# First attention of a decoder block: order of the masked reads, of the e-transposes and of the rstd work around two state scans

## The reference, cut to what matters

```python
q, k, v = heads(x @ Wq, 64), heads(x @ Wk, 64), heads(x @ Wv, 128)
s = clip(heads(x @ Ws, 64), -32, 32)
# scan over t: hk = hk * g_t + k_t p_t ;  ok_t = q_t . hk
pv = softmax(ok)                                   # over the 64 slots
# scan over t: hv = hv * g_t + p_t v_t ;  ov_t = pv_t . hv
o = ov * rsqrt(mean(ov * ov, -1) + 1e-5) * g_norm_weight
o = o * (g * sigmoid(g))                           # g = x @ Wg
out = o @ Wo                                       # added to x, then a layer norm
```

## Time and profile before

| | us |
|---|---|
| three runs | 971.32, 976.60, 978.88 |
| median | 976.6 |
| profiled execution, whole | 978.59 |
| its span (first to last instruction) | 976.7 |

### The profile page before, as it was taken

How to read it: one execution, slowest core, us unless ns; L and a number is a source line. 1 busy time by engine, 2 the same in 40 slices (tenths; PEclk the granted TensorE clock), 3 DMA queues, 4 the chain that set the end, 5 groups by cost and what they waited for, 6 DMA issues and landing times.

```text
span 976.7 us, 15390 instructions
## 1 busy us (share of the span) xinstructions
PE 870.8 (89%) x5247; PEld 569.4 (58%) x5251; DVE 716.3 (73%) x1389; ACT 505.8 (52%) x1020; POOL 407.7 (42%) x338
## 2 busy tenths in 40 slices
PE   7999999999999999989999999999547867999886
PEld 3466666656566666656867776676423654443443
DVE  5677786959686877769765556665577798997897
ACT  3563554545444445445443334455522457898485
POOL 0202448494847667454214343343477303221012
PEclk9999999999999999998799999999866998999998
DMA  5450212211230222100746999999633000000001
GB/s 191 159 194 28 65 49 87 70 66 61 74 103 33 87 71 87 40 5 1 228 141 209 314 314 316 317 302 289 183 92 97 17 1 3 7 7 6 1 6 38
DMA packets 54743, 106.46 MB, mean 109 GB/s; under 512 B 8909, under 2 KB 26645, under 8 KB 54165
## 3 DMA queue, kind: packets, MB, share of 16 engines
q1 hardware_dynamic: 48917, 89.88, 29.4%
q0 software_dynamic: 5760, 15.74, 5.9%
HBM read 88.45 MB, written 17.14 MB: 108 GB/s over the span
## 4 chain that ended last, share of the span: by engine, by line
PE 61%; DVE 17%; DMA 6%; ACT 5%; issue 5%; POOL 3%; SPq 2%; DVEq 0%; ACTq 0%; POOLq 0%
PE ps L785 10%; PE ps L723 7%; PE ps L969 6%; PE ps L881 5%; PE ps L981 4%; PE ps L733 4%; DVE row_max L2757 3%; POOL key_part L1545 3%; PE ps L1317 3%; DVE state L2177 2%; DMA w_dn<-in_w_dn 2%; PE ps L803 2%; DMA y_dram<-y_out 2%; PE ps L1303 2%; PE ps L847 1%
## 5 line engine op out<-in xcount | busy, mean ns | idle before, releaser
L1516 POOL DMA_INDIRECT xg<-x_dram,tok_of x68 | 65.1, 958 | 129.1 <-PE ps L1042 91.4
L785 PE MATMUL ps<-w_vg,xT 128*128 128x512 f32 x256 | 116.8, 597 | 1.2 <-DVE th L2220 1.2
L1466 POOL TENSOR_TENSOR state<-state,rows_bc 128x1024 f32<-128x1024 f32 x22 | 53.8, 2444 | 95.5 <-DVE state L2177 41.9
L723 PE MATMUL ps<-xT,w_qks 128*128 128x512 f32 x192 | 86.6, 596 | 5.9 <-ACT qT L1623 5.3
L969 PE MATMUL ps<-w_gv,xgT 128*128 128x352 f32 (+1 forms) x272 | 87.7, 464 | 2.8 <-DMA w_dn<-in_w_dn 2.7
L2757 DVE TENSOR_REDUCE row_max<-ps 128x4 f32<-128x1024 f32 x64 | 74.4, 1217 | 7.1 <-PE ps L1282 6.3
L2188 DVE TENSOR_TENSOR aT<-ps,tri 128x768 f32<-128x768 f32 x64 | 59.7, 954 | 27.0 <-PE ps L733 26.9
L1623 ACT ACTIVATE probT<-ps 128x512 f32<-128x512 f32 x128 | 69.5, 594 | 10.3 <-PE ps L1303 9.8
L785 PEld LDWEIGHTS ps<-w_vg,xT 128*128 128x128 f32 x256 | 45.8, 190 | 48.8 <-issue 43.1
L981 PE MATMUL ps<-w_dn,hidT 88*128 88x256 f32 (+1 forms) x272 | 69.9, 379 | 0.0
L969 PEld LDWEIGHTS ps<-w_gv,xgT 128*128 128x128 f32 x272 | 48.8, 190 | 27.2 <-issue 5.6
(11 more groups left out here) (328 smaller groups left out, 2064.8 us busy)
## 6 DMA issues: line engine op xcount, KB each, us to landing
w_gv<-in_w_gv SPq DMA_DIRECT2D x68, 352.0 KB, 7.1
rows_bc<-x_dbl_dram SPq DMA_DIRECT2D x32, 512.0 KB, 3.8
w_dn<-in_w_dn SPq DMA_DIRECT2D x68, 192.0 KB, 8.8
y_dram<-y_out SPq DMA_DIRECT2D x68, 128.0 KB, 7.0
y_dram<-blank SPq DMA_DIRECT2D x4, 1408.0 KB, 13.2
w_vg<-in_wvg SPq DMA_DIRECT2D x8, 512.0 KB, 4.9
w_qks<-in_wqks SPq DMA_DIRECT2D x8, 384.0 KB, 3.1
w_o<-in_wo SPq DMA_DIRECT2D x8, 256.0 KB, 2.7
```

The costliest lines, as they stand in the source:

```text
L723: last = mm(bank(PJ + n % 2), w_qks[:, k, part * P:(part + 1) * P], xT[:, k, half * 512:(half + 1) * 512], start=(k == 0), stop=(k == KD - 1))
L785: last = mm(bank(PJ + t % 2), xT[:, k, t * P:(t + 1) * P], w_vg[:, k, :], start=(k == 0), stop=(k == KD - 1))
L1466: G.tensor_tensor(state_of(m), state_of(m), c_row[:, n % 2], ALU.mult).then_inc(read_out, 1)
L1516: G.indirect_dma_start(xg[:, j, :], None, x_dram, bass.IndirectOffsetOnAxis(ap=col, axis=0)).then_inc(gathered[j], 16)
```

## The change

Six edits:

- the reads go to banks AB, Y, PJ, AB (`MASK_BANK`); three reads stand in a row, then mix 0, read 3, mixes 1 to 3. The wait for the last gate moves from read 1 to read 2, and read 1 waits for both halves of `wT` (its bank pair Y held their source);
- VectorE's masks read from the same banks;
- the transposes of the next pair's `eT` (`turn_e`) move from the start of the next step to between its second and third scores; step 0 makes its own. Their wait for `const_loaded` goes;
- ScalarE: decay gated, copy 0, `rms`, copy 1, decay clip, copies 2 and 3;
- VectorE: scan masks2 moves behind the sums of squares and the joining operation, ahead of the wait for rstd;
- no computing instruction is added or left out, and GpSimd's and SyncE's programs stay as they are.

```diff
--- before.py
+++ after.py
@@ -172,6 +172,7 @@
 
         ps = ctx.enter_context(nc.psum_tensor("ps", [P, 8, 512], F32))
         PJ, AB, X, Y = 0, 2, 4, 6
+        MASK_BANK = (AB, Y, PJ, AB)
 
 
         xres = sb("xres", [P, TILES, D])
@@ -762,11 +763,8 @@
                     mm(bank(AB + half), dt_w[:, e * P:(e + 1) * P], x_dbl[0:DR, half * 512:(half + 1) * 512],
                        start=True, stop=True).then_inc(scan_mm, 1)
 
-            def step(i, last_pair):
-
+            def turn_e(i):
                 pe.wait_ge(eT_ready, at(i, 2, 2))
-                pe.wait_ge(const_loaded, 48)
-
                 pe.wait_ge(mixed_added, at(i, 4, 1))
                 for n in range(2):
                     for t in range(4):
@@ -774,6 +772,9 @@
                         last = nc.tensor.transpose(ps[:, X + n, t * P:(t + 1) * P], eT[:, c:c + P], ident[:])
                     last.then_inc(e_turned, 1)
 
+            def step(i, last_pair):
+                if i == 0:
+                    turn_e(0)
                 pe.wait_ge(vg_loaded, at(i, 16, 16))
 
                 def project_vg(t):
@@ -829,13 +830,13 @@
                 project_vg(TILES - 1)
 
                 def read(b):
-                    if b % 2 == 0:
-                        pe.wait_ge(wT_copied, at(i, 2, b // 2 + 1))
-                    if b == 1:
+                    if b < 2:
+                        pe.wait_ge(wT_copied, at(i, 2, b + 1))
+                    elif b == 2:
                         pe.wait_ge(gate_ready, at(i, 8, 8))
-                    if b >= 2:
-                        pe.wait_ge(read_masked, at(i, 4, b - 1))
-                    both_heads(PJ if b % 2 else AB, eT, wT, b).then_inc(read_ready, 1)
+                    else:
+                        pe.wait_ge(read_masked, at(i, 4, 1))
+                    both_heads(MASK_BANK[b], eT, wT, b).then_inc(read_ready, 1)
 
                 def mix(b):
                     pe.wait_ge(read_masked, at(i, 4, b + 1))
@@ -851,12 +852,12 @@
 
                 if i == 0:
                     pe.wait_ge(scan_act, 12)
-                read(0)
-                read(1)
-                for b in range(B):
+                for b in range(3):
+                    read(b)
+                mix(0)
+                read(3)
+                for b in range(1, B):
                     mix(b)
-                    if b + 2 < B:
-                        read(b + 2)
                 if not last_pair:
                     project_qks(i + 1, False, range(4))
 
@@ -892,7 +893,9 @@
                     if b + 2 < B:
                         turn(b + 2)
                 if not last_pair:
-                    scores(i + 1, range(B))
+                    scores(i + 1, range(2))
+                    turn_e(i + 1)
+                    scores(i + 1, range(2, B))
 
 
             pe.wait_ge(scan_consts, 48)
@@ -1713,10 +1716,12 @@
                     act.wait_ge(o_ready, at(i, 4, b + 1))
                     f(sq_of(b).rearrange("p a b -> p (a b)"), bank(X + b), ACT.Square).then_inc(squares_ready, 1)
                 decay_at(i, "gated")
+                if not last_pair:
+                    copy_qk(i + 1, range(1))
+                rms(i)
+                if not last_pair:
+                    copy_qk(i + 1, range(1, 2))
                 decay_at(i, "clip")
-                if not last_pair:
-                    copy_qk(i + 1, range(2))
-                rms(i)
                 if not last_pair:
                     copy_qk(i + 1, range(2, 4))
                 if i == 0:
@@ -2262,11 +2267,10 @@
                 gate(7)
                 for b in range(B):
                     dve.wait_ge(read_ready, at(i, 4, b + 1))
-                    mask(b, PJ if b % 2 else AB).then_inc(read_masked, 1)
+                    mask(b, MASK_BANK[b]).then_inc(read_masked, 1)
                 if i == 0:
                     exp_plus_one()
                 scan_at(i, "masks")
-                scan_at(i, "masks2")
                 for b in range(B):
                     dve.wait_ge(squares_ready, at(i, 4, b + 1))
                     V.tensor_reduce(ss[:, 4 * b:4 * b + 4], sq_of(b), AX.X, ALU.add).then_inc(squares_read, 1)
@@ -2274,6 +2278,7 @@
                 dve.wait_ge(vec_step, at(i, CHAIN, 4))
                 V.scalar_tensor_tensor(out=ss[:], in0=ss[:], scalar=1.0 / DV, in1=eps, op0=ALU.mult,
                                        op1=ALU.add).then_inc(squares_read, 1)
+                scan_at(i, "masks2")
                 dve.wait_ge(rstd_ready, at(i, 1, 1))
                 for b in range(B):
                     for t in range(2):
```

## The result

The changed kernel takes 964.37 us (median of 10 runs, 960.54 to 970.25) against 976.09 (10 runs of the kernel before beside it, 971.32 to 978.88). The ratio is 0.989, with a 95% interval of 0.9867 to 0.9912: faster by 1.1%. I had forecast 966.5. The profiled execution took 967.34, with a span of 965.5 us, against 976.7 in the kernel before.

A forecast was written before the change was run, and what follows sets the result against it. TensorE bounds, with about 1.6 us a step in gaps. Step 0 +0.1, step 1 -1.5, five steps -7.25, last pair -1.7: -10.35 from 976.7 gives 966.3, median 966.5; likeliest case 963 to 972, leaving out 2 in 10 962 to 987.

The forecast's parts named there:

- The border rule: At the border of GpSimd's two drives, VectorE's waiting first scan goes in, starting near 218.8 and ending 221.0.
- Drives keep their turn: Rival, chance 0.25: the first scan waits for both GpSimd drives; +2.4 us a step, 987 us in all.
- no collision: Rival, chance 0.09: scans are not held, or hold without cost; 1.88 us a step gained, 964 us in all.
- all three collisions: VectorE's first scan waits for a drive, the third for y until 230.6, the fourth for the next drive until 234.95.
- The race lost: Rival, chance 0.13: the first scan misses the drives' border, later races are won; +0.9 us a step, 978 us.
- Reads and mixes: TensorE from first read to next projection: 8.95 us instead of 9.70, by a hidden gate wait and fewer shape changes.
- Queries' copies: TensorE's 0.88 us wait for ScalarE's copy goes, as copy 0 stands behind one decay needing only the first scan.
- The turn between the scores: Transposes of eT fill TensorE's 0.37 us wait between scores, less about 0.15 for another shape change: net 0.22.
- The wait at `project_out(2)`: TensorE newly waits 0.4 us a step for VectorE's addition of head 0, wanted at 237.46 and had at 237.9.
- Steps 2 to 6: The five like steps of the attention: 1.45 us gained in each, 7.25 in all.
- Last pair: Attention's last head pair: reads 0.8 us earlier and one decay less before gating; 1.7 us gained.
- The failed term: Step 1, with no early drive in the way and the same second and third collision: 1.5 us gained.

The follow-up runs named there:

- reads and transposes: The changed kernel with scan masks2, the rstd work and ScalarE's order put back as before: 979.83 us, ratio 1.0034 to the kernel before.
- the changed kernel's second six runs: The changed kernel unaltered, measured again beside the version with two further VectorE reorderings, on the same chip: 965.68 us, ratio 0.9898.
- the third part: Scan masks2 behind the sums of squares, with ScalarE's new order; alone on the kernel before: 978.41 us, ratio 1.0011.
- reads: The kernel before with only the new banks and order of the reads: 967.89 us, ratio 0.9931.
- rstd: The kernel before with only ScalarE's new order and VectorE's scan masks2 behind the sums: 978.41 us, ratio 1.0011.
- the one drive on 64 columns: The changed kernel with GpSimd's drive for the front scan computed on 64 of 1024 columns: 965.54 us in one execution, steps of 50.73.
- all three products on 64 columns: The changed kernel with the front scan's drive and the masks scan's C row and y on 64 columns: 966.74 us in one execution.

## Why the prediction was right, and where it was not

**The border rule.** The whole forecast stood on one reading of the earlier trace rows, that a scan which waits goes in between two drives that GpSimd has ready. It does: second drive 4.35 long (6.69 for two, less 2.34), first scan 2.89. "Drives keep their turn" (987 us) falls, and so does "no collision", as all three collisions came. "The race lost" is what the kernels without the moved transposes show, 0.35 to 0.4 us on the wrong side; with them the margin that I had put at 0.43 was 0.7, an error of estimated terms that happened to fall on the good side. The Trainium skill (SBUF — State Buffer, Who interferes with whom) has whoever issues first hold the pair for the whole instruction; the trace agrees, down to the 64-column product of 2.31 us.

**Reads and mixes.** 8.95 forecast, 8.67 measured (211.11 to 219.78): 1.03 gained instead of 0.75 to 0.8. The miss is in the reads in a row: the three take 2.16 us up to mix 0 (211.11 to 213.27), where the sum had 0.76 + 0.76 + 0.86 = 2.38. The rest came as summed: 1.54 for mix 0 and the change back, and 4.97 instead of 5.03 for what follows.

**Queries' copies.** 0.88 forecast, gained whole. The gain was right, its condition was missing: it needs the held drive to be covered by the sums of squares. With the scans in a row as before, the copy would have been later than ever (2.25, reads and transposes).

**The turn between the scores.** Net 0.22 forecast: the wait of 0.37, less 0.15 for the change of shape. From `project_out(2)` to the next value projection lie 7.69 instead of 8.18 us (236.46 to 244.15; the earlier trace rows): 0.49, so no price of the change of shape is to be seen there. From that projection to read 0, 0.10 is lost again (18.63 instead of 18.53). Net 0.39.

**The wait at `project_out(2)`.** Forecast 0.4 us, measured 1.0. It is a difference of two times, and each was off: by the working TensorE wanted it 24.69 us behind read 0 and got it at 25.13; in the trace it wanted it at 24.35 (mostly the reads, which gave more than forecast) and got it at 25.35, 0.15 behind the addition's end at 25.20. The path runs through VectorE here, so what TensorE gained more, it waited more. That the step's length came out within 0.06 us is luck in part: `project_out(2)` came 0.22 later than forecast, and the turn between the scores gave 0.17 more.

**Steps 2 to 6:** 1.45 forecast, 1.39 measured. **Last pair:** 1.7 forecast, 1.91 measured: from read 0 to the gating 10.93 us (417.76 to 428.69) instead of 12.95, and TensorE waits there for VectorE, as forecast, 3.27 us instead of 4.27.

**The failed term is step 1.** I gave it -1.5 us, and -0.22 came. The lag of 1.02 us for VectorE's softplus work I had, and the wait grew by just that, 1.21 to 2.23; it was booked as eaten up by the reads of step 0 and was. What I had put at nothing, without a reason, is what TensorE's clock does after such a wait. The trace of the kernel before had a sign of it: its clock stands at 0.50 from 440 to 444 us, behind the last pair's wait of 4.27. In step 1 of the changed kernel:

```profile
93.97 5.40 PE L786 MATMUL ps<-w_vg,xT 128*128 128x512 f32 x8 [2.23 <-DVE th L2225]
```

Before, the same eight matmuls took 3.70 behind a wait of 1.21, and the work to the second next piece 4.41 us (94.13 to 98.54); now it is 6.11 (93.97 to 100.08): 1.7 us of half clock, against 1.9 gained elsewhere in the step. By the forecast's own terms (-0.16, -0.22, -6.95, -1.91) the sum is -9.24 against -10.35, short by 1.1; this term alone is short by 1.3, the others together over by 0.2. The profiled span then came out near the forecast since the work behind the attention took 1.9 us less in that execution, which is scatter. The median too moved further (11.7 us) than the attention explains (9.3), so the closeness of 964.37 to the forecast of 966.5 hides the term that failed; beside the changed kernel's second six runs the medians differ by 9.5.

## What to carry to other kernels

When two engines exclude each other for whole instructions, a border between two instructions is where the other side gets in, on both sides: put short independent work that the other engine doesn't hold (here the sums of squares) between two scans, so that the product which was let in is over by the next. Parts of a change that set such a race can't be judged alone: here -0.5, 0 and +0.9 us a step made -1.4 together, and reads with transposes, without the third part, +1.6, all of it TensorE's clock at half behind the longer wait. Where a change lengthens a single wait of TensorE, price the clock behind it too.

## What the runs showed of the hardware

- A scan held by a GpSimd product ends 2.28 us behind that product's recorded end less 0.13; a product held by a scan 2.36 less 0.2. With either engine's next instruction ready, the one of the other engine that waits goes first (reads with transposes: 2.88, then the drive, then 4.38).
- A GpSimd product of 128x64 took 0.32 us alone and 2.31 held by a scan: its row then shows the wait and hardly the work.
- TensorE's granted clock went to half, 0.50, behind a wait of 2.23 us for the gate in step 1 and stayed at 1.00 behind one of 1.21 at the same place, and behind the waits of 1.40 (reads) and 1.6 us (rstd) in steps 2 to 6. With the one drive on 64 columns it stayed at 1.00 behind 2.24 too; with all three products on 64 columns it fell. Behind the waits of 2.24 to 2.27 us for the queries' copy it fell in two of five steps in one kernel (5.40 us for eight matmuls against 3.70) and in all five in another, with waits of 2.23 to 2.27. Behind the last pair's wait of 3.27 or 4.27 it fell in every trace. So a wait of 2.25 us has no fixed price: 2.25 us, or 4 us with the clock's part. What decides it I can't say from these runs.
